# A fused attention and expert layer: rotary projections in four buffers, max tiles from step 6, a shorter routing and another order inside a head

## What is computed

```
x  = L0_attn_hidden_states            # (1, 2048, 256)
xn = _layernorm(x)
# attention
q, k, v = proj(Wq, bq), proj(Wk, bk), proj(Wv, bv)      # 16 heads of 16
q, k = _apply_rope(q, sin, cos), _apply_rope(k, sin, cos)
scores = q @ k.T / 4, keys outside [0,205) and [1536,2048) masked out
attn = softmax(scores) @ v ; out = attn @ Wo.T + bo
# experts
logits = xn @ router_w.T ; top_vals, top_idx = top_k(logits, 2)
expert, weight = top_idx[:, 0], softmax(top_vals)[:, 0]
act = silu(gate) * up ; y = weight * (down_w[expert] @ act)
return x + out + y
```

## Time and profile before

| | |
|---|---|
| median of three runs | 416.41 us (415.82 to 417.6) |
| profiled execution | 417.95 us |
| its span in the profile | 416.1 us |
| TensorE busy | 376.5 us (90%) |
| VectorE busy | 323.8 us (78%) |
| ScalarE busy | 265.0 us (64%) |
| GpSimd busy | 65.7 us (16%) |

### The profile page before, as it was taken

How to read it: one execution, slowest core, us unless ns; L and a number is a source line. 1 busy time by engine, 2 the same in 40 slices (tenths; PEclk the granted TensorE clock), 3 DMA queues, 4 the chain that set the end, 5 groups by cost and what they waited for, 6 DMA issues and landing times.

```text
span 416.1 us, 12241 instructions
## 1 busy us (share of the span) xinstructions
PE 376.5 (90%) x4646; PEld 189.4 (46%) x4646; DVE 323.8 (78%) x549; ACT 265.0 (64%) x537; POOL 65.7 (16%) x82
## 2 busy tenths in 40 slices
PE   0884989979898999999999999999999999998896
PEld 0553445646565444444444444444444444442265
DVE  5769287797763788888888888878888888884666
ACT  2622255754344677777778777777887777788920
POOL 5005242232200003303123032030000000000000
PEclk9999799999999899999999999999999999999999
DMA  7997244455411211213123032131120210246716
GB/s 250 406 395 167 54 132 142 148 179 169 112 54 51 67 49 47 71 27 93 43 57 89 13 89 66 29 94 33 38 62 20 58 56 17 69 134 99 156 49 205
DMA packets 30920, 42.53 MB, mean 102 GB/s; under 512 B 10724, under 2 KB 25700, under 8 KB 30048
## 3 DMA queue, kind: packets, MB, share of 16 engines
q1 hardware_dynamic: 29000, 36.71, 30.6%
q0 software_dynamic: 1872, 5.11, 4.8%
HBM read 27.75 MB, written 13.67 MB: 100 GB/s over the span
## 4 chain that ended last, share of the span: by engine, by line
PE 77%; DVE 11%; ACT 5%; issue 4%; DMA 3%; SPq 0%; ACTq 0%; DVEq 0%; POOLq 0%
PE ps L714 22%; PE ps L696 20%; PE ps L642 17%; PE ps L589 4%; PE ps L752 3%; PE ps L602 3%; PE ps L541 2%; ACT probs L1251 2%; DMA o_st<-sorted_rows,token_of 2%; PE ps L628 2%; DMA x_sb<-x_in 1%; DVE parts L959 1%; DVE mx L996 1%; PE ps L503 1%; PE ps L497 1%
## 5 line engine op out<-in xcount | busy, mean ns | idle before, releaser
L1002 DVE TENSOR_REDUCE mx<-ps 128x1 f32<-128x717 f32 x232 | 198.9, 899 | 37.4 <-PE ps L642 35.2
L714 PE MATMUL ps<-q_op,k_op 98*32 98x512 bf16 (+1 forms) x1472 | 131.2, 384 | 7.5 <-ACT probs L1251 5.7
L642 PE MATMUL ps<-k_op,q_op 96*32 96x512 bf16 (+1 forms) x1856 | 118.7, 317 | 0.8 <-ACT ys L1218 0.7
L1251 ACT ACTIVATE probs<-ps 128x512 f32<-128x512 f32 x192 | 99.2, 602 | 24.4 <-PE ps L714 24.3
L642 PEld LDWEIGHTS ps<-k_op,q_op 96*32 96x32 bf16 x1856 | 53.8, 96 | 74.1 <-issue 34.9
L714 PEld LDWEIGHTS ps<-q_op,k_op 98*32 98x32 bf16 (+1 forms) x1472 | 40.5, 95 | 64.6 <-ACT probs L1251 25.6
L696 PE MATMUL ps<-probs,v_op 128*32 128x512 f32 x384 | 50.1, 595 | 0.2 <-ACT o_st L1242 0.2
L1251 ACT ACTIVATE dn<-ps 77x512 f32<-77x512 f32 x64 | 34.9, 597 | 10.9 <-PE ps L714 10.9
L1251 ACT ACTIVATE gu<-ps 128x512 f32<-128x512 f32 x64 | 33.0, 602 | 10.6 <-PE ps L714 10.6
L1251 ACT ACTIVATE wqk<-ps 128x512 f32<-128x512 f32 x64 | 33.0, 602 | 10.6 <-PE ps L714 10.6
L445 POOL DMA_INDIRECT o_st<-sorted_rows,token_of x23 | 26.1, 1135 | 82.2 <-PE ps L575 52.5
(11 more groups left out here) (118 smaller groups left out, 371.2 us busy)
## 6 DMA issues: line engine op xcount, KB each, us to landing
q_parts<-parts SPq DMA_DIRECT2D x12, 256.0 KB
sorted_results<-ys SPq DMA_DIRECT2D x23, 128.0 KB
q_op<-q_parts SPq DMA_DIRECT2D x15, 192.0 KB
gu<-gu_in SPq DMA_DIRECT2D x1, 2816.0 KB
tab<-tab_in SPq DMA_DIRECT2D x1, 2048.0 KB, 11.5
sorted_rows<-xn SPq DMA_DIRECT2D x4, 512.0 KB, 7.0
out<-x_sb SPq DMA_DIRECT2D x8, 256.0 KB, 2.4
q_op<-q_parts SPq DMA_DIRECT2D x15, 128.0 KB
```

Source lines behind the costliest of these rows:

```text
L642: ins = pe.matmul(ps[r:r + CW, at + c0:at + c0 + n], q_op[slot][0:KR, P * t + r:P * t + r + CW], k_op[slot][0:KR, c0:c0 + n], start=True, ...
L714: ins = pe.matmul(bank(4 + u % RING)[r:r + w, :], k_op[k][:, c0 + r:c0 + r + w], q_op[k][:, QB * b:QB * b + QB], start=True, stop=True)
L1002: dve.tensor_reduce(mx[:, slot, t:t + 1], ps[:, at:at + NK], AX.X, ALU.max).then_inc(max_reduced, 1)
L1251: act.activation(prob[c][0:rows, QB * b:QB * b + QB], bank(4 + u % RING)[0:rows, :], ACT.Exp, scale=SCALE).then_inc(exp_done, 1)
```

## The change

- **Rotation buffers.** Four for two: besides the two in `probs`, the two halves of `xn`. `biased(u)` waits for `lowest(u-4)`, and for units 2 and 3 for the stores of `xn`. Units 2 and 3 and the first half of 4 are projected before step 0, the other three halves in steps 0 to 2. VectorE's and ScalarE's rows for the units are spread by hand over steps 0 to 12.
- **Max tiles.** One a step in steps 6 to 12, two in 13 to 19, one each in 20, 23 and 24. `TURN_AT` is 18, and the transposed maxima stand in another PSUM bank.
- **Routing.** Maximum and comparison read PSUM; ties are broken by a scan that counts matches within a token (`count`, `same_token`) for a product and a second maximum. The ranks use PSUM bank 1 for 7. The V additions stand behind the token list.
- **SyncE and GpSimd.** Stores and loads are issued in other steps; the gather of results also waits for the last `lowest`.
- **Heads.** `ORDER` has six different sections. Head 0's first S waits for the last `ys`, its third for the last early reduction.

```diff
-ORDER = 2 * ("MSSMSSMP" + "MSSMSSMP" + "MSSMSSP")
+ORDER = ("MSMSSSMP" + "MSMSSSMP" + "SMMSSP" + "SMSMSSSMP" + "MSMSSSMP" + "SMMSSSP")
-TURN_AT = 16
-EARLY_AT = {8: (None, 0), 9: (None, 1)}
-EARLY_AT.update({9 + n: (2 * n, 2 * n + 1) for n in range(1, 3 * NT // 4)})
+TURN_AT = 18
+EARLY_AT = {6 + n: (None, n) for n in range(7)}
+EARLY_AT.update({13 + n: (7 + 2 * n, 8 + 2 * n) for n in range(7)})
+EARLY_AT.update({20: (None, 21), NSLOT: (22, None), NSLOT + 1: (23, None)})
...
-        rot = probs[:, :, :].rearrange("p r (a n) -> p r a n", a=4)
+        rot = [half.rearrange("p (a n) -> p a n", a=4) for half in (
+            probs[:, 2, :], probs[:, 1, :], xn[:, 0:NT // 2, :].rearrange("p t d -> p (t d)"),
+            xn[:, NT // 2:NT, :].rearrange("p t d -> p (t d)"))]
...
             pool.wait_ge(route_ready, 1)
+            pool.wait_ge(lo_ready, NPROJ)
...
             for c in V_ORDER[:2]:
                 project_v(c)
-            pe.wait_ge(rank_read, 1)
+            pe.wait_ge(logits_read, 1)
             project(1)
-            project_v(V_ORDER[2])
             pe.wait_ge(slot_ready, 1)
...
-            for c in V_ORDER[3:]:
+            for c in V_ORDER[2:]:
                 project_v(c)
+            for u in (2, 3):
+                project(u)
...
                 if n == NT:
                     pe.wait_ge(qk_loaded, 2 * LOADS)
-                    pe.wait_ge(neg_copied, 1)
...
+                if s == TURN_AT:
+                    pe.wait_ge(ys_ready, s - 2)
+                    turn_neg(0, 0, early_turned_neg)
                 if s in PROJECT_IN:
                     u, odd = PROJECT_IN[s]
                     project(u, (odd,))
+                if s == TURN_AT + 1:
+                    pe.wait_ge(neg_copied, 1)
...
-                if s == TURN_AT:
-                    turn_neg(0, 0, early_turned_neg)
...
-            PROJECT_IN = {0: (2, 1), 1: (3, 0), 2: (3, 1), 3: (4, 0), 4: (4, 1), 5: (LAST, 0), 6: (LAST, 1)}
+            PROJECT_IN = {0: (4, 1), 1: (LAST, 0), 2: (LAST, 1)}
...
-            project(2, (0,))
+            project(4, (0,))
...
+                        if first and u == 0:
+                            pe.wait_ge(ys_ready, NSLOT)
+                        if first and u == RING - 1:
+                            pe.wait_ge(max_reduced, len(EARLY_TILES))
...
-            pe.wait_ge(ys_ready, NSLOT)
...
-            dve.tensor_copy(te["logit"][:].rearrange("p (b j) e -> p j b e", b=NQB),
...
-            step(dve.tensor_tensor(te["rev"][:], te["best"][:], rev, ALU.mult))
             settle()
-            step(dve.tensor_reduce(tk["pick"][:], te["rev"][:], AX.X, ALU.max))
-            settle()
-            settle()
-            dve.tensor_tensor(by_token[0], over_experts(tk["pick"][:]), rev, ALU.is_equal).then_inc(hot_ready, 1)
+            dve.scalar_tensor_tensor(by_token[0], te["count"][:], 1.0, te["best"][:], ALU.is_equal, ALU.mult
+                                     ).then_inc(hot_ready, 1)
             dve.wait_ge(hot_ready, 1)
             dve.tensor_tensor_scan(upto[:], later[:], hot[:], 0.0, ALU.mult, ALU.add).then_inc(upto_ready, 1)
+            dve.tensor_copy(by_block("logit"), logits).then_inc(logits_read, 1)
...
+                if before == NT - 1:
+                    negate(0, 0)
...
-                if after == NT - 1:
-                    negate(0, 0)
...
+                if s == 0:
+                    rest(1)
+                    times_cos(2)
+                    times_sin(2)
+                elif s == 1:
+                    turn(2)
+                    lowest(1)
+                    rest(2)
                     weights()
...
+                elif s == 12:
+                    lowest(LAST)
...
-                if u >= 2:
-                    act.wait_ge(lo_ready, u - 1)
-                act.activation(rot[:, ROT_SLOT[u], 1 + 2 * odd, 0:n], proj_bank(u, odd), ACT.Identity,
+                if u in (2, 3):
+                    act.wait_ge(xn_stored, 16 * 4)
+                if u >= 4:
+                    act.wait_ge(lo_ready, u - 3)
+                act.activation(rot[u % 4][:, 1 + 2 * odd, 0:n], proj_bank(u, odd), ACT.Identity,
                                bias=bqk[:, col:col + 1], scale=1.0).then_inc(proj_read, 1)
...
-            BIASED_AT = {2 * n: n + 2 for n in range(LAST - 1)}
-            HIGH_AT = {2 * n + 1: n + 1 for n in range(LAST)}
-            MID_AT = {2 * n: n for n in range(NPROJ)}
+            BIASED_IN = {0: (4, 0), 1: (4, 1), 2: (LAST, 0), 3: (LAST, 1)}
+            HIGH_AT = {1: 2, 3: 3, 5: 4, 10: LAST}
+            MID_AT = {0: 1, 4: 3, 6: 4, 11: LAST}
...
             highest(0)
+            for odd in range(2):
+                biased(2, odd)
+            middle(0)
+            for odd in range(2):
+                biased(3, odd)
             copy_rows(0)
```

More of the change, by code:

```diff
@@ L130, in layer @@
         tk = {n: sb("tk_" + n, [P, NT]) for n in
-              ("top", "pick", "second", "gap", "ratio", "denom", "weight", "row")}
+              ("top", "second", "gap", "ratio", "denom", "weight", "row")}
         before_me = o_st[2][:, 0:P]
@@ L250, in rot_of @@
         def rot_of(u, first):
-            r, n = ROT_SLOT[u], PROJ[u][2]
-            return rot[:, r, first:4:2, 0:n]
+            return rot[u % 4][:, first:4:2, 0:PROJ[u][2]]
         block = ctx.enter_context(nc.Block())
@@ L975, in _ @@
             second_best()
-            dve.wait_ge(ones_ready, RING + 1)
-            dve.wait_ge(wv_in, 32)
-            for n in range(2):
-                add_bv(n)
             copy_token_of()
@@ L985, in _ @@
             turn(0)
-            for n in range(2, NCH):
+            dve.wait_ge(ones_ready, RING + 1)
+            dve.wait_ge(wv_in, 32)
+            for n in range(NCH):
                 add_bv(n)
+            rest(0)
             times_cos(1)
             times_sin(1)
-            rest(0)
+            lowest(0)
+            turn(1)
             def early_reduce_tile(n):
@@ L1210, in expert_step @@
                     copy_rows(s + 1)
-                if s in MID_AT:
-                    middle(MID_AT[s])
+                if s == 0:
+                    highest(1)
+                if s == 2:
+                    middle(2)
+                if s in BIASED_IN:
+                    biased(*BIASED_IN[s])
                 if s >= 2:
@@ L1222, in expert_step @@
                     highest(HIGH_AT[s])
-                if s in BIASED_AT:
-                    for odd in range(2):
-                        biased(BIASED_AT[s], odd)
+                if s in MID_AT:
+                    middle(MID_AT[s])
             for u in range(2):
```

106 lines of the change are left out of this document (63 added, 43 removed).

## The result

| | before | changed |
|---|---|---|
| median in this comparison | 416.12 us (415.7 to 417.6) | 404.64 us (403.97 to 405.43) |
| profiled execution, its span | 417.95, 416.1 us | 404.71, 402.9 us |

The ratio is 0.9745 (95% interval 0.9705 to 0.9785): 10.6 us less, between 8.9 and 12.3. Two later comparisons gave 0.9762 (0.971 to 0.9814) and 0.9751 (0.9703 to 0.98). The forecast was 404.3.

A forecast was written before the change was run, and what follows sets the result against it. Bounds: the gather wait, the steps' VectorE-ScalarE-TensorE turn-taking, and 16 heads of 16.18 us. Terms 6.7 + 1.2 + 0.7 + 3.5 = 12.1 us, from 416.4, gave 404.3 us; range 401 to 409.5.

The forecast's parts named there:

- The start of 45.3 us: Step 0's gate/up start, forecast at 45.3 instead of 45.87 us with the gather wait filled by projections.
- gives nothing by itself: Routing: token list about 1.1 us sooner, but no gain alone, since TensorE has other work until the gather lands.
- 0.6 us sooner: Step 0 at 45.3 instead of 45.87 us, with four more projection halves done; included in the 6.7 us.
- The walk: Steps 0 to 13 followed instruction by instruction: step 14 starts at 95.8 instead of 102.47 us, 6.7 us sooner.
- The loop of the earlier trace: Projection steps: `lowest` frees a buffer, `biased` fills it, then TensorE goes on; two steps took 9.59 us.
- The transpose's 1.2 us: Steps 14 to 24: TensorE's 1.20 us wait at the transpose of the negated maxima disappears.
- step 20's tile and the start of head 0: One tile instead of two in step 20 gains 0.3 us; only head 0's first S waiting for `ys` gains 0.4.
- a walk that gave 0.30: Late heads: sections 3 and 6 lose no wait, the others about 0.16 us each; 15.84 us instead of 16.16.
- the term of 3.5: Heads' new order: 0.25 us a head for the 14 heads with M rows, 3.5 us in all.
- Rival 1: Steps keep their pace near 9.6 us a pair through ScalarE's order, casts ahead of tanh: 410.4 us; chance 0.12.
- Rival 2: TensorE's clock falls to 0.50 in steps 3 to 7, four steps of 5.2 us, +5: 409.3 us; chance 0.10.
- one of the signs that were to show the prediction wrong: A granted clock under 0.9 in steps 3 to 7 was listed as showing the prediction wrong.

The follow-up runs named there:

- routing_back: The changed kernel with the six-operation routing of before and two V additions ahead of the token list again: 406.0 us (before: 414.7).
- order_alone: The kernel before with only the new ORDER of the heads: 411.58 us (before: 414.7).
- filler_behind_down: The changed kernel with three more unread fp32 matmuls on TensorE behind the down projection in each of steps 3, 4 and 5: 404.97 us.
- casts_later: The changed kernel with five ScalarE casts (highest of units 4, 5; middle of 3, 4, 5) moved behind the next step's tanh and row copy: 400.97 us.
- tiles_old: The changed kernel with the old placing of the early max tiles and the negation behind the last reduction: 405.66 us (before: 414.7).
- old_order: The changed kernel with the ORDER of the heads from before: 408.49 us (before: 416.29).
- clock_kept: The kernel before with unread matmuls on TensorE: six in the gather wait, two each in steps 23 and 24, one ahead of head 0: 412.47 us (before: 415.05).

## Why the prediction was right, and where it was not

**Routing, gap, start of step 0.** The start of 45.3 us was right (45.25), so were the 43.3 for the first tile (43.31) and the full clock. The sentence that the routing "gives nothing by itself" was wrong: by routing_back it gives 0.5 us, through the wait for `hot` and not through the gather. And "0.6 us sooner" compares with a late gather. In order_alone step 0 came 17.80 us after the routing began; the changed kernel takes 21.43 always. Where the gather lands early, step 0 starts 3.6 us later than before, with four more halves projected.

**Steps 0 to 13.** The walk forecast 6.7 us; the profiled rows give 6.9, and no start was off by more than 0.8 us. Its reason holds too. TensorE is not the bound (filler_behind_down), and the waits behind casts were real (casts_later): 1.33 us four times, 0.19 twice and 0.58 for `highest(1)`, where I had 1.35, 0.25 and 0.6. The loop of the earlier trace rows is gone: `biased` (L1207), which waited 1.12 us for `lowest` there, waits for VectorE in no row of steps 0 to 3, here the last one:

```profile
58.77 0.71 ACT L1207 ACTIVATE probs<-ps,bqk 128x512 f32<-128x512 f32 x1
```

No run puts the two buffers back alone, so how the gain divides between the buffers, the four halves projected ahead of step 0 and the new order of rows stays open. Over the whole way the comparison is less kind: from the routing to step 14 the changed kernel takes 71.75 us, before 78.75 in its profile but 73.76 in order_alone, whose program is the same there. Steps themselves (B) gain 5.6 us at a full clock.

**Steps 14 to 24.** The transpose's 1.2 us: the pair of steps around it is 1.25 shorter (6.79 for 8.04). For step 20's tile and the start of head 0 I took 0.3 + 0.4, and the rows gave 1.12 us: 0.39 and 0.73. The term that I had put at nothing is the fall of the clock at the head of head 0, 1.3 us in the profiles; the prediction has it only as something that could come on top. With the tiles in steps 23 and 24 TensorE works 1.71 of 2 us where it was 1.4:

```profile
122.00:124.00 2.00, 1.71 (x10) 1.14 (x10) 1.49 (x3) 0.75 (x3) 0.00 (x0) 1.00 0.06 21
```

That the clock holds because of them is not shown: tiles_old has none there, works 1.49 and 1.35 of 2 us from 122 to 126, and its clock held as well.

**Heads.** 0.25 us a head, from a walk that gave 0.30: a late head measured 0.22. I had taken all 14 for late ones; by VectorE's reciprocal rows the first seven after head 0 take 16.77 us before and 16.61 now (287.10 - 169.71 and 275.48 - 159.21, by seven), 0.16 less each. So the term of 3.5 was too large: 2.7 in the two profiles, with the last heads in it, and 3.2 and 3.1 by the medians of the two runs on the order. In the walk, sections 3 and 6 run without a wait as it says (2.12 and 2.34 us, the bare sums of their rows). Section 4, the one with the transpose, loses 0.21 us and section 5 loses 0.19, where I had 0.16: the transpose's weight load starts at 315.98, just behind the end of the negated maxima (315.69 + 0.17). That it waits for them I read from these times, and have not tested.

**Rival 1** did not come: steps 4 and 5 took 8.6 us together, steps 6 and 7 7.3, not 9.6. **Rival 2** came in part: the clock fell to about 0.55 in step 5, and step 5's gate/up took 2.40 us. It cost nothing, since I had priced it as if TensorE set the pace; the rival's price of 5 us was wrong even where its condition was met. With it came one of the signs that were to show the prediction wrong, a granted clock under 0.9 in steps 3 to 7 (0.61 and 0.54): it was no such sign.

**The sum.** That 404.3 lies 0.3 us from the measured 404.64 is in part luck: two errors cancel. The terms were read from an execution of 417.95 us and subtracted from a median of 416.41, 1.5 less. And their sum was too small: between the two profiles the rows give 6.9 + 1.25 + 1.12 + 1.3 + 2.7 = 13.2 us (to rounding) where the sum had 12.1, because the heads were put 0.8 too high while 1.3 for the clock at head 0 and some 0.7 in smaller terms were missing. The mechanisms stand, the walk of a head for late heads alone.

As a difference between typical executions 12.1 is too much, and 10 to 11 is what the comparisons show: the kernel before has a median of 414.6 us over the 48 executions of the table by clock, because its time depends on how often its clock falls and when its gather lands. The stretches can be added up for its best case, a full clock and an early gather: B is 5.6 us shorter (55.96 to 50.32), C 2.3 (33.04 and 33.24 to 30.86), D 2.2 (278.5 to 276.3, the 3 us of the order less some 0.7 which old_order's 279.20 shows to be lost there in the changed kernel), and A 3.6 longer (17.80 to 21.43). That is 6.5 us, and the kernel before at a mean clock of 1.000 does take 411.6 us, 6 to 7 more than the changed one (404.7 to 405.6). The other 3 to 4 us of the measured gain are what the kernel before loses on average to a late gather and to falls of the clock. How they divide, the runs show only roughly: clock_kept, without the falls, gained 2.4 (by its interval 1.0 to 3.8).
